# Spreading the output norm's reciprocal roots: four transposes on TensorE, or a store and a broadcast load on SyncE's queue

## What is computed

```
def _L0_xattn_ref(q, k, v, Wq, Wk, Wv, Wo, bo, g):
    ...
    out = jnp.einsum('bcn,oc->bon', out, Wo) + bo[None, :, None]
    norm = jnp.maximum(jnp.sqrt(jnp.sum(out * out, axis=1, keepdims=True)), 1e-12)
    return out / norm * g * np.sqrt(DIM)
...
x = x + jnp.tanh(g_xattn[0]) * _L0_xattn_ref(_layernorm(x, axis=-1), ctx_4096, ctx_4096, ...)
x = x + jnp.tanh(g_ffn[0]) * _L0_ffn_ref(_layernorm(x, axis=-1), L0_ffn_w_gate, L0_ffn_w_up, L0_ffn_w_down)
```

## Time and profile before

| | |
|---|---|
| median of 3 runs | 1387.82 us (1387.11 to 1389.66) |
| span of the profiled execution | 1386.2 us |
| PE busy | 1314.9 us, 95% |
| DVE busy | 1003.7 us, 72% |
| ACT busy | 634.1 us, 46% |
| POOL busy | 580.5 us, 42% |
| SP's DMA queue | 232.9 MB, its packets take 67.3% of 16 engines' span |

### The profile page before, as it was taken

How to read it: one execution, slowest core, us unless ns; L and a number is a source line. 1 busy time by engine, 2 the same in 40 slices (tenths; PEclk the granted TensorE clock), 3 DMA queues, 4 the chain that set the end, 5 groups by cost and what they waited for, 6 DMA issues and landing times. The chain is left out here.

```text
span 1386.2 us, 30208 instructions
## 1 busy us (share of the span) xinstructions
PE 1314.9 (95%) x12408; PEld 961.9 (69%) x12408; DVE 1003.7 (72%) x1343; ACT 634.1 (46%) x879; POOL 580.5 (42%) x357
## 2 busy tenths in 40 slices
PE   4787599999999899999999999999999999999999
PEld 2454387855787558876598757885598748985994
DVE  6977778878799976887688875889578866641330
ACT  4668786853544424453434533453344443320220
POOL 0249925866274472444334451346034432240120
PEclk8998799999999999999999999999999999999999
DMA  9939999896664879778777975787677895663421
GB/s 352 408 145 336 267 288 306 243 184 151 146 163 99 174 180 244 182 181 186 168 176 174 196 187 136 200 169 186 150 184 181 179 171 130 159 173 88 138 76 46
DMA packets 401417, 260.00 MB, mean 188 GB/s; under 512 B 325312, under 2 KB 342080, under 8 KB 401280
## 3 DMA queue, kind: packets, MB, share of 16 engines
q1 hardware_dynamic: 394368, 232.90, 67.3%
q10 hardware_dynamic: 6912, 25.17, 5.7%
HBM read 152.37 MB, written 25.95 MB: 129 GB/s over the span
## 5 line engine op out<-in xcount | busy, mean ns | idle before, releaser
L1118 PE MATMUL ps<-w_dn,inter_buf 128*128 128x512 fp8e4 x1376 | 307.8, 380 | 2.0 <-DVE inter_buf L1372 1.3
L1118 PEld LDWEIGHTS ps<-w_dn,inter_buf 128*128 128x128 f16 x1376 | 134.9, 99 | 157.8 <-issue 4.7
L1804 POOL TENSOR_TENSOR qs<-qs,q_stat 128x1024 f32<-128x1024 f32 x64 | 129.6, 2024 | 232.9 <-DVE q_stat L1615 232.9
L1034 PE MATMUL ps<-zT,w_gu 128*128 128x256 f16 x1664 | 191.2, 274 | 3.0 <-DVE zT L1372 2.4
L1034 PEld LDWEIGHTS ps<-zT,w_gu 128*128 128x128 fp8e4 x1664 | 163.0, 99 | 29.2 <-DVE zT L1372 2.6
L1069 PE MATMUL ps<-w_gu 128*128 128x128 f16 x2880 | 174.0, 219 | 2.7 <-DVE w_gu L1715 1.8
L1069 PEld LDWEIGHTS ps<-w_gu 128*128 128x128 fp8e4 x2880 | 165.8, 98 | 7.1 <-issue 3.1
L1860 POOL TENSOR_TENSOR w_gu<-w_gu 128x512 f32<-128x512 f32 x60 | 82.4, 1373 | 179.8 <-DVE w_gu L1715 112.6
L1069 PE MATMUL ps<-zT,w_gu 128*128 128x128 f16 x2176 | 132.6, 219 | 0.0
L1715 DVE SCALAR_TENSOR_TENSOR w_gu<-ps,w_gu 128x512 f32<-128x512 f32 x120 | 82.5, 688 | 68.0 <-PE ps L1069 67.9
L1069 PEld LDWEIGHTS ps<-zT,w_gu 128*128 128x128 fp8e4 x2176 | 125.5, 98 | 3.9
(11 more groups left out here) (195 smaller groups left out, 2588.8 us busy)
## 6 DMA issues: line engine op xcount, KB each, us to landing
w_gu<-forms SPq DMA_DIRECT2D x158, 256.0 KB, 3.0
ct_raw<-forms SPq DMA_DIRECT2D x52, 256.0 KB, 3.1
w_dn<-in_down_w SPq DMA_DIRECT2D x19, 512.0 KB, 6.0
xb<-in_x ACTq DMA_DIRECT2D x16, 512.0 KB, 6.8
x_dram<-xb SPq DMA_DIRECT2D x16, 512.0 KB, 3.9
fin<-x_dram SPq DMA_DIRECT2D x32, 256.0 KB, 2.9
out<-fin SPq DMA_DIRECT2D x32, 256.0 KB, 2.4
inter_buf<-in_up_w SPq DMA_DIRECT2D x15, 512.0 KB, 9.7
```

Source lines behind the costliest of these rows:

```text
L1034: last = nc.tensor.matmul(ps[:, rest_bank(g, j), s * T:s * T + T], w_gu[:, w, k, :], zT[:, h, k, :], start=(k == 0 and h == 0), stop=(k == ...
L1118: mm = nc.tensor.matmul(ps[:, down_bank(g, k), :], inter_of(g, j, u % 2, b), w_dn[:, j, hf * 512:hf * 512 + 512], start=(u == 0), stop=(u ...
L1804: nc.gpsimd.tensor_tensor(v, v, q_stat[:, u % 2, 1, :].unsqueeze(2).broadcast_to([P, 2 * HEADS, DH]), ALU.mult).then_inc(q_prob, 1)
```

## The change

For batches 0 to 3 the norm stays as it was. From batch 4 on (`BY_DMA`), `R` is gone. In its place SP issues two DMAs for each half: `put_r` stores `rsv` (128 x 4 numbers, 2 KB) as one row of a new DRAM tensor, and `get_r` waits for that store to land and loads the row into every partition of sq, whose square has been used up by then. `x2m` reads sq with a stride of four numbers instead of the bank `OUT`. `rs` waits for the store of the same half of the batch before, no longer for its transposes. `OUT` is free again after `ssg`. All step numbers from about the 680th on are new, with the first change in PE's order at step `kt(4, 2)`, ahead of `ctxk(3, 1)`; up to there PE's order is the same.

```
+BY_DMA = 4
...
-    "outp": (8, 0, B), "yev": (2, 0, B), "ss": (2, 0, B), "ssg": (2, 0, B), "rs": (2, 0, B), "R": (2, 0, B),
+    "outp": (8, 0, B), "yev": (2, 0, B), "ss": (2, 0, B), "ssg": (2, 0, B), "rs": (2, 0, B), "R": (2, 0, BY_DMA),
+    "put_r": (2, BY_DMA, B), "get_r": (2, BY_DMA, B),
...
+    "put_r": [1087, 1127, 1328, 1387, 1567, 1634, 1752, 1804, 1929, 1988, 2173, 2218, 2334, 2422, 2601, 2671, 2811,
+        2856, 3002, 3092, 3189, 3232, 3371, 3471],
+    "get_r": [1109, 1146, 1329, 1395, 1577, 1637, 1757, 1813, 1952, 2002, 2176, 2235, 2379, 2423, 2609, 2674, 2816,
+        2864, 3026, 3106, 3210, 3246, 3410, 3474],
...
+            def put_r(i, hf):
+                wait(sp, rs_ready, 2 * i + hf + 1)
+                sp.dma_start(r_dram[2 * i + hf, :].rearrange("(p k) -> p k", p=P), rsv[:, hf, :]).then_inc(r_stored, 16)
+
+            def get_r(i, hf):
+                wait(sp, r_stored, 16 * (2 * (i - BY_DMA) + hf + 1))
+                sp.dma_start(sq, r_dram[2 * i + hf:2 * i + hf + 1, :].broadcast_to([P, 512])).then_inc(r_in, 16)
...
             def x2m(i, hf):
-                wait(dve, r_ready, 2 * i + hf + 1)
                 wait(dve, y_ready, 2 * i + hf + 1)
                 if i == 0:
                     dve.wait_ge(coef_x, 1)
+                if i >= BY_DMA:
+                    wait(dve, r_in, 16 * (2 * (i - BY_DMA) + hf + 1))
+                    v = y.rearrange("c (k p) -> c k p", k=4)
+                    nc.vector.scalar_tensor_tensor(out=v, in0=sq.rearrange("c (p k) -> c k p", k=4),
+                                                   scalar=small[:, COEF_X:COEF_X + 1],
+                                                   in1=v, op0=ALU.mult, op1=ALU.mult).then_inc(y_scaled, 1)
+                    return
+                wait(dve, r_ready, 2 * i + hf + 1)
...
             def rs(i, hf):
                 wait(pool, ss_guarded, 2 * i + hf + 1)
-                wait(pool, r_ready, 2 * i + hf - 1)
+                wait(pool, r_ready, min(2 * i + hf - 1, 2 * BY_DMA - 1 + hf))
+                if i > BY_DMA:
+                    wait(pool, r_stored, 16 * (2 * (i - BY_DMA) + hf - 1))
```

More of the change, by code:

```diff
@@ L175 @@
-    "turn_q": [479, 525, 661, 709, 785, 839, 918, 943, 964, 984, 1074, 1100, 1129, 1175, 1334, 1365, 1395, 1427, 1538,
-        1586, 1623, 1660, 1732, 1764, 1825, 1866, 1933, 1953, 2017, 2071, 2153, 2180, 2220, 2247, 2346, 2376, 2439,
-        2493, 2575, 2602, 2642, 2669, 2768, 2798, 2861, 2915, 2997, 3024, 3064, 3091, 3184, 3210, 3271, 3326, 3371,
-        3413],
-    "outp": [180, 182, 185, 186, 241, 244, 248, 249, 334, 337, 340, 344, 402, 406, 409, 413, 650, 652, 653, 657, 747,
[6 rows of a table removed]
-    "yev": [192, 256, 361, 418, 664, 759, 919, 965, 1077, 1130, 1335, 1396, 1539, 1622, 1733, 1799, 1934, 1979, 2154,
[3 rows of a table removed]
@@ new lines @@
+    "kexp": [27, 29, 99, 115, 170, 183, 221, 225, 280, 373, 413, 443, 509, 643, 650, 683, 739, 808, 912, 917, 1030,
+        1063, 1101, 1141, 1178, 1269, 1286, 1370, 1407, 1470, 1471, 1575, 1737, 1773, 1805, 1811, 1934, 1944, 1961,
+        1962, 2110, 2190, 2210, 2246, 2343, 2344, 2374, 2388, 2552, 2584, 2616, 2662, 2793, 2794, 2807, 2821, 2968,
+        3027, 3063, 3090, 3209, 3225, 3253, 3254],
+    "ktr": [67, 80, 123, 139, 190, 207, 238, 263],
+    "k_f": [73, 100, 128, 146, 193, 213, 258, 270],
@@ new lines @@
+    "turn_k": [387, 439, 477, 513, 566, 666, 723, 776, 859, 881, 956, 983, 1082, 1122, 1208, 1209, 1314, 1315, 1354,
+        1394, 1450, 1511, 1578, 1625, 1746, 1788, 1819, 1826, 1924, 1979, 2010, 2040, 2175, 2192, 2199, 2240, 2367,
+        2406, 2436, 2462, 2548, 2633, 2666, 2684, 2827, 2848, 2860, 2879, 2962, 3041, 3088, 3113, 3183, 3229, 3240,
+        3270],
+    "ctxk": [105, 153, 217, 276, 455, 557, 710, 828, 948, 1019, 1172, 1257, 1358, 1437, 1580, 1655, 1816, 1863,
+        1986, 2070, 2224, 2276, 2438, 2470, 2654, 2709, 2858, 2916, 3084, 3129, 3288, 3329],
@@ new lines @@
+    "qf_lo": [479, 520, 565, 708, 783, 841, 882, 934, 961, 979, 1009, 1096, 1136, 1162, 1237, 1363, 1398, 1421,
+        1475, 1549, 1590, 1670, 1708, 1754, 1820, 1868, 1913, 1956, 2017, 2079, 2132, 2180, 2225, 2270, 2351, 2370,
+        2460, 2524, 2568, 2598, 2661, 2731, 2776, 2796, 2903, 2939, 2970, 3037, 3065, 3114, 3176, 3204, 3326, 3340,
+        3386, 3426],
+    "turn_q": [484, 524, 662, 714, 787, 843, 953, 954, 960, 1011, 1077, 1112, 1138, 1163, 1316, 1353, 1377, 1413,
+        1556, 1574, 1644, 1658, 1734, 1756, 1821, 1846, 1903, 1936, 2071, 2103, 2163, 2185, 2230, 2247, 2326, 2385,
+        2471, 2517, 2573, 2623, 2673, 2712, 2801, 2830, 2884, 2904, 2987, 3030, 3087, 3119, 3173, 3207, 3293, 3322,
+        3359, 3444],
@@ new lines @@
+    "outp": [181, 184, 187, 189, 241, 244, 248, 249, 334, 340, 346, 351, 405, 410, 412, 414, 651, 652, 656, 657,
[6 rows of a table added]
+    "yev": [191, 256, 362, 417, 663, 758, 914, 940, 1058, 1137, 1344, 1408, 1516, 1610, 1732, 1808, 1943, 1955,
[3 rows of a table added]
+    "ssg": [202, 265, 368, 429, 672, 764, 930, 978, 1066, 1134, 1349, 1410, 1515, 1619, 1733, 1803, 1954, 1987,
[4 rows of a table added]
+    "ld_xr": [19, 151, 364, 606, 971, 1236, 1517, 1518, 1946, 2081, 2380, 2410, 2750, 2841, 3215, 3299],
[9 rows of a table added]
+    "zt_hi": [359, 474],
+    "zt_lo": [363, 487],
+    "z_hi": [855, 984, 1250, 1465, 1806, 1882, 2014, 2287, 2487, 2711, 3123, 3168, 3476, 3477],
@@ new lines @@
+    "form": [291, 1106, 1107, 1119, 1157, 1170, 1174, 1200, 1275, 1281, 1282, 1308, 1330, 1332, 1333, 1334, 1415,
+        1416, 1484, 1485],
+    "load_form": [1536, 1537, 1545, 1546, 1548, 1564, 1571, 1572, 1573, 1597, 1606, 1607, 1608, 1609, 1630, 1635,
[11 rows of a table added]
+    "product": [1550, 1560, 1562, 1563, 1568, 1583, 1584, 1595, 1596, 1604, 1605, 1623, 1624, 1656, 1664, 1671,
[11 rows of a table added]
+    "evict": [1533, 1534, 1535, 1543, 1544, 1565, 1582, 1592, 1593, 1615, 1616, 1621, 1627, 1626, 1628, 1646, 1667,
[11 rows of a table added]
+    "pair_mul": [1547, 1629, 1653, 1669, 1682, 1728, 1748, 1749, 1830, 1831, 2082, 2091, 2092, 2100, 2109, 2115,
[3 rows of a table added]
@@ L800, in _ @@
                      "turn_k": turn_k, "turn_q": turn_q, "turn_z": turn_z, "turn_zs": turn_zs, "store_form": store_form,
[L801 removed]
+                     "load_form": load_form, "put_r": put_r, "get_r": get_r, "st_x2": st_x2, "reload": reload,
                      "st_out": st_out})
```

244 lines of the change are left out of this document (103 added, 141 removed), and 191 rows, old and new, of the table WHEN.

## The result

The changed kernel takes 1371.95 us (median of 4 runs, 1369.67 to 1375.11) beside 1387.46 us for the kernel before on the same chip: ratio 0.9893, 95% interval 0.9875 to 0.9911. As a share of 1387.8 us that is 14.8 us less, between 12.4 and 17.3. The medians themselves are 15.5 us apart. The prediction had 9.8 less.

What follows compares the result with a forecast made beforehand. Behind the opening, TensorE's instruction stream plus some 9 us of gaps was taken as the bound. -10.6 + 0.8 = -9.8, and 1387.8 - 9.8 = 1378.0 us; forecast band 1373 to 1383, range 1370 to 1389.

Steps and rivals of the forecast that it cites:

- main term: TensorE, batches 4 to 15: 96 transposes removed, four per half at 0.44 us, 24 x 0.44 = 10.6 us less.
- Rival A: TensorE's waits from 275 us on: the new order also closes all 9.4 us of old gaps, 1367.8 us; chance 0.06.
- round trip: From the end of the sums through `rs`, store and load until sq is filled: 7.0 us, or 13.4 with a slow store.
- headroom: Time after `ss` that VectorE's queue ahead of `x2m` still waits for TensorE work: 0 to 16.4 us over 24 halves.
- rival D: Broadcast late at VectorE's `x2m`: at a 12 us trip, 23 to 39 us lost, 1401 us with 23; chance 0.10.
- turn_q(8, 3): Transpose on SyncE's queue, needed by `outp(8, 1, 0)`: lands late behind blocked steps, TensorE loses 0.8 us.
- a queue with air: SyncE's queue: 246.1 us in 144 waits for products ahead of its ring loads, though it can hold up later steps.
- B: TensorE's transposes: each costs its duration, 279 ns, so 26.8 us are saved, 1361.0 us; chance 0.02.
- C: Hand-overs between engines: the new order opens some ten gaps of 1 us each, gain gone, 1386 us; chance 0.12.
- E: TensorE's stream: another instruction remains for each half, or none is gone; no size, given no chance.

Runs made afterwards that it cites:

- e3_new_order_transposes: The kernel before, all its TensorE transposes kept and no store or load, in the changed kernel's step order: 1382.85 us, ratio 0.9969.
- e4_one_more_hop: The changed kernel with one more DMA per half, copying the stored row to a second DRAM row, and one more SyncE wait: 1395.65 us, ratio 1.0057.
- e9_dmas_beside: The kernel before, in its own order, plus the stores, broadcast loads into a buffer nobody reads, and their waits: 1412.50 us, ratio 1.0177.
- e1_old_order: The changed kernel with the step order (table WHEN) of the kernel before: 1500.47 us, ratio 1.0822.

## Why the prediction came out as it did

**The direction and the main term were right, the total was not quite.** The measured 1371.95 us lies inside the outer range (1370 to 1389) but just below the band of the forecast (1373 to 1383). By the ratio it is 1373.0, at the band's edge. The main term, 24 x 0.44 = 10.6 us, was measured as 9.1 and 10.9. The choice of the distance in the earlier trace rows over the busy time and over the duration was the step that mattered. The Trainium skill (TensorE: Matmul & The Clock Gate, Part 4: PE-mode transpose) gives about 275 ns for a transpose; as a duration the traces agree (a mean of 279 ns for 128 before; of the 32 that are left the median is 273, the mean 313), as a cost per transpose the medians of these runs give 0.095 to 0.114 us.

**The term that failed is the order: set at 0 with one loss of 0.8 us, it gave 4.3 us back (2.5 to 6.2).** I had followed only what the new order might break and taken all of the earlier trace rows as it was. Rival A had the sign right but not the size (9.4), and its counter-argument, that nine gaps of nine causes don't all close, held: the waits in `e3_new_order_transposes` are 7.9 us, only 1.5 less, and the larger part of the 4.3 us has no place in the traces yet. With -10.6 - 4.3 the sum is -14.9, and the measured ratio gives -14.8. That it fits to 0.1 us is luck, since each part is known to 2 us at best.

**The round trip was under-sized: 7.0 us predicted, 10.6 measured.** Medians over 24 halves, behind the end of the sums: `rs` starts at 0.5 (0.4 predicted), the store is issued 1.5 us behind that (1.3), the load 3.2 behind the store (2.4), and it lands 4.2 later (2.9). Medians don't add up: taken for each half as a whole, the load is issued at 6.4, and 6.4 + 4.2 = 10.6. The load is the largest miss, and I had priced it by `fin<-x_dram` in the earlier trace rows. The order isn't what makes it slow: in the old order it landed in 3.9 to 4.2 us as well. The store, which I had feared most, was right at 2.3 us (median; 9.7 at the one place above). The Trainium skill (DMA: Bandwidth & Descriptors, Specifications) says that pieces under 512 B cost a read-modify-write, as a limit on line rate. The median store of 16 B pieces here shows little above the fixed cost of about 2 us in its section Latency and other measured facts; its rule on the rate is not tested by 2 KB.

**Yet the longer trip cost nothing measurable, and that was luck: the headroom was under-sized as well.** I had VectorE wait at three halves before the last for 6.7 us together. It waited at three before the last for 5.8 us (0.73, 1.91, 3.13) and at the last for 4.43. The two sums agree by chance. A trip of 10.6 us against my six headrooms of 3.6 to 7.7 us would have been at least 27 us of waiting before the last half. But I had counted only TensorE's work ahead of `x2m`. In the trace VectorE has other things to do, and apart from the last half and one at 7.8 us it reaches `x2m` no earlier than 10.0 us behind the sums. Two of the three waits, 0.73 and 1.91 us, are at halves where the load landed 15 us or more behind the sums, in part since the store took 4.9 and 9.7 us to land. `x2m` starts 13.1 us (median) behind the sums in the changed kernel, later than the landing at 10.6. I had put the point at which the gain is eaten (rival D) at a round trip of 9 to 10 us, which is wrong: at 10.6 nothing measurable was lost. For 12 us I had 23 us of loss and 1401, and `e4_one_more_hop`, at 12.0, lost 23.7 and gave 1395.65. The mechanism holds, and its threshold lies further out, between 10.6 and 12.0. The agreement in price is weak evidence, since SyncE's extra wait has a part in that run, which the 23 us had not.

**SyncE.** 48 issues and their waits cost TensorE only at `turn_q(8, 3)`, which the prediction named: 0.8 us predicted, 3.3 to 3.5 in two traces. The size was off because its issue took 8.66 us instead of 1.8. The 1.8 was one row besides: over the 56 issues of `eT` before, the median is 2.5 us, over those of `kT` 2.9. That the queue has air held in this order only. SyncE's waits in the changed kernel, then the same wait for products as the first of them in `e3_new_order_transposes`, which has the order and no store or load:

```profile
SPq L791 <- PE ps L1088: 90.1, 73, 6.4
SPq L795 <- POOL rsv L1838: 60.5, 18, 16.5
SPq L799 <- DMA r_dram<-rsv: 20.0, 11, 3.0
SPq L783 <- PE ps L1072: 116.1, 78, 11.0
```

The waits for `rs` are longer here (60.5 us) than in `e9_dmas_beside` (36.9), yet they cost less. Of the 246.1 us of the earlier trace rows the order alone leaves 116.1; the store and the load take it to 90.1. The waits for `k` and `p`, ahead of the transposes, fall in the same step from 107.9 and 90.2 to 83.6 and 56.0 us, so the new waits took the air of these three. In the old order the same two waits, with their transfers, cost 24.7 us. My argument by "a queue with air" was thus not enough by itself; that I had followed the queue step by step in the new order was.

**`x2m`** takes 1.14 us (median) instead of the predicted 0.95, 31.8 us for 24 in this trace. VectorE's total fell all the same (1003.7 to 979.2 us), but by the order: from 275 us on it is 788.1 us before, 745.0 with the order alone and 760.7 with the change. Beside TensorE's stream the longer product costs nothing that can be measured.

**Rivals B, C and E** did not occur: no duration as a cost, ten gaps of 1 us were not opened (the two waits in the list above at 2.2 and 3.6 us are what came anew), and the transposes are gone. C's own sum was off: ten places at 1 us each are 1388, not 1386.

## What to carry to other kernels

Price a removed TensorE instruction by its distance from start to start on the path, not by its duration or its busy row. A wait put into an in-order queue is priced by what is queued behind it and by when that is due: the same instructions took 1372 us in an order laid out for the wait, with the product 13 us behind the sums, and 1500 us in the old one. Moving the product alone is not enough: 12 us behind the sums in the old order gave 1458 us. When a diff also re-orders the work, look at the gaps it may close with the same care as at those it may open, and test order and mechanism in separate kernels, each alone.

## What the runs showed of the hardware

- A store of 2 KB in 128 pieces of 16 B from SBUF to DRAM landed in 2.3 us (median; 1.9 to 2.6 over all traces, 9.7 at most), where one of 256 KB in the same kernel took 3.0.
- The issue of one DMA transpose on SyncE's queue took 1.3 to 8.7 us, with a median of 2.2 to 3.0 in every trace. What stands behind it on the queue was issued only when it was over.
- The form loads' median landing is 4.0 us in the new order without any broadcast (`e3_new_order_transposes`), and 3.2 in the old order with the stores and loads (`e9_dmas_beside`), against 3.0 before. It is the order that slows them, not the 24 broadcasts.
- Idle time of TensorE in the middle of the kernel cost clock too: 14.3 busy us of 20 at a granted 0.74, and 43 us over the whole of `e1_old_order`. Behind single waits of 2 to 3 us it cost some 1.7 us in some executions and nothing in others of the same program.
- The first 255 us, with the same instructions, differ by up to 6.7 us (253.0 to 259.7) between executions of different kernels.
